# Attention with residual and layer norm on one core: splits of a coming quad's input in other graphs, and a bias add placed earlier on GpSimd

## Chip, cores and metric

The kernel runs on one core of one Trainium2 chip. The metric is the device time of one execution in microseconds (us). Some durations below are in nanoseconds where the profile has them so.

## The reference

For each of 128 graphs with 128 nodes and 384 features (12 heads of 32), all in float32:

```python
q = x @ Wq.T;  k = x @ Wk.T;  v = x @ Wv.T + bv          # split in 12 heads
a = softmax(where(all(a == 0), -inf, q k^T * 384**-0.5 + adj))   # NaN rows become 0
y = x + (a @ v) @ Wo.T + bo
out = (y - mean(y)) / sqrt(var(y) + 1e-5)                # over the 384 features
```

## The kernel before

The work goes in **quads** of four graphs, 32 of them, over tiles with two buffers (quad parity `p`). A hardware loop (`over_quads`) runs 15 times over a pair of quads, and the last pair is written out behind it. Each engine has its own instruction stream, in an order written out by hand, and semaphores order the engines among each other. Within a quad, `graph(j, p, b, ...)` for b = 0 to 3 is what an engine does in graph b's time. It works on several graphs at once: output projection, residual and layer norm of graph b, transposes of the probabilities of graph b+1, and softmax of graph b+2 (`later`). `nxt` is the next quad, `aft` the one after it.

The projections are exact to float32 by a split: a matrix is a high part (rounded, type fp32r) and a low part (the rest), and a product is three matmuls for each chunk of 128 features, hi·hi, hi·lo and lo·hi (`split_product`, L217 to L219). The input xT of a quad comes by one DMA into `xT_raw` (one buffer, three chunks). ScalarE makes the high parts (`keep_xT_hi`, L384), VectorE the low ones by a subtraction that reads `xT_raw` and `xT_hi` (`keep_xT_lo`, L501). Both are made for the quad `aft` during the present one.

The steps that matter here, by engine:

- **TensorE** (`quad`): ahead of `project_qk(*aft, 0, 1)`, near the end of graph 2's work, it waits for all three xT_lo and for `y_read` of graph 2, because that product writes the bank which the residual of graph 2 reads. Likewise `project_qk(*nxt, 3, 0)`, behind `project_v(j, p, 3, 1)`, waits for graph 0's `y_read`. `scores(*nxt, 0)` waits for the copy of product 5 (`qk_done`). Line L266 is `attend`, L241 `scores`, L254 the transposes.
- **ScalarE** (`graph`): exponentials (`exp_trio`, L402), copies of the products (`keep_qk`, L395), of the transposed probabilities (`keep_pT`, L409), of the attended values (`keep_oT_hi`, L415), and the high parts.
- **VectorE** (`graph`): `keep_oT_lo` (L562), the biased scores of four trios (`bias_trio`, L525), `keep_v` (L515), then `mask_half(0)`: `neg_sum` from `fold` (L537), reciprocal (L542), `live` (L547, reads two SBUF tiles), `row_scale` (L553, reads two SBUF tiles). Then `residual` (L569, gives `y_read`), `statistics`, `mean_variance`, `add_eps` (L582), `normalise` (L589, waits for GpSimd's `inv_std`), and `mask_half(1)`.
- **GpSimd** (`graph`): two `fold_half` (L661), which wait for the biased scores, `scale_half` 0 (L668), which waits for `row_scale`, `inverse_std` (L675), which waits for `add_eps`, `add_bo` (L654), which adds the output bias to the next graph's x and, except for the first graph of a quad, waits for nothing, and `scale_half` 1.
- **SyncE** issues all DMAs in one queue: output stores as they are done, and the loads of a coming quad between them.

In the notes below a "turn" is the passage from the end of the loop's body back to its start.

Of the kernel before, what the change touches and what calls it, by code (L numbers as in the profile page):

```python
# [28 lines left out]
QUAD = 4  # L29
# [16 lines left out]
def attention_kernel(nc, x, xT, adj, wq_t, wk_t, wv_t, wo_t, bv, bo, out):  # L46
# [7 lines left out]
    with ctx:  # L54
# [324 lines left out]
        @block.scalar  # L379
        def _(act):  # L380
            def keep_xT_hi(j, p, c):

                act.wait_ge(xT_loaded, 16 * (2 * j + p) + 16)
                nc.scalar.activation(xT_hi[p][:, c, :], xT_raw[:, c, :], ACT.Copy).then_inc(xT_hi_done, 1)  # L384

            def keep_w_hi(part):

                cols, factor = W_PARTS[part]
                act.wait_ge(w_loaded[cols.start // HIDDEN], 16)
                nc.scalar.activation(w_hi[:, :, cols], w_raw[:, :, cols], ACT.Copy, scale=factor)\  # L390
                    .then_inc(w_hi_done, 1)

            def keep_qk(j, p, k, turn):
                act.wait_ge(qk_psum, QK * (2 * j + p) + k + 1)
                nc.scalar.activation(qkT[p][:, k, :], turn_bank[turn][:, :], ACT.Copy)\  # L395
                    .then_inc(qk_done, 1)

            def exp_trio(j, p, b, trio):

                act.wait_ge(neg_a_done, 4 * (QUAD * (2 * j + p) + b) + trio + 1)  # L400
                for u in range(CHUNKS * trio, CHUNKS * (trio + 1)):
                    last = nc.scalar.activation(probs[b % 2][:, u, :], neg_a[b % 2][:, u, :], ACT.Exp,  # L402
                                                bias=neg_max[b % 2][:, u:u + 1], scale=-1.0,
                                                accum_out=row_sum[b % 2][:, u:u + 1])
                last.then_inc(exp_done, 1)

            def keep_pT(j, p, b, trio):
                act.wait_ge(pT_psum, 4 * (QUAD * (2 * j + p) + b) + trio + 1)
                nc.scalar.activation(pT[:, CHUNKS * trio:CHUNKS * (trio + 1), :],  # L409
                                     pT_bank[trio % 2][:, 0:HIDDEN].rearrange("p (c n) -> p c n", c=CHUNKS),  # L410
                                     ACT.Copy).then_inc(pT_done, 1)

            def keep_oT_hi(j, p, b):
                act.wait_ge(oT_psum, QUAD * (2 * j + p) + b + 1)
                nc.scalar.activation(oT_hi[:, :, :],  # L415
                                     turn_bank[ATTEND_BANK[b]][:, 0:HIDDEN].rearrange("p (c n) -> p c n", c=CHUNKS),
                                     ACT.Copy).then_inc(oT_hi_done, 1)

            def graph(j, p, b, has_next, has_after):
                nxt, aft = ahead(j, p, 1), ahead(j, p, 2)  # L420
                turn = 1 - ATTEND_BANK[b]
                more = b + 1 < QUAD or has_next
                more2 = b + 2 < QUAD or has_next
                if b == 1 and has_next:
                    keep_qk(*nxt, 3, turn)
                if b == 3 and has_after:
                    keep_qk(*aft, 0, turn)
                keep_oT_hi(j, p, b)
                if more:
                    keep_pT(*later(j, p, b, 1), 0)  # L430
                    keep_pT(*later(j, p, b, 1), 1)
                if more2:
                    exp_trio(*later(j, p, b, 2), 0)
                    exp_trio(*later(j, p, b, 2), 1)
                if b == 1 and has_next:
                    keep_qk(*nxt, 4, turn)
                if b == 3 and has_after:
                    keep_qk(*aft, 1, turn)
                if b == 2 and has_after:
                    keep_xT_hi(*aft, 2)  # L440
                if more2:
                    exp_trio(*later(j, p, b, 2), 2)
                if more:
                    keep_pT(*later(j, p, b, 1), 2)
                    keep_pT(*later(j, p, b, 1), 3)
                if more2:
                    exp_trio(*later(j, p, b, 2), 3)
                if b == 0 and has_after:
                    act.wait_ge(v_psum, QUAD * (2 * j + p) + QUAD)
                    keep_xT_hi(*aft, 0)  # L450
                if b == 1 and has_next:
                    keep_qk(*nxt, 5, turn)
                if b == 3 and has_after:
                    keep_qk(*aft, 2, turn)
                if b == 1 and has_after:
                    keep_xT_hi(*aft, 1)

            def quad(j, p, has_next, has_after):
                for b in range(QUAD):
                    graph(j, p, b, has_next, has_after)  # L460

            for c in range(CHUNKS):
                keep_xT_hi(0, 0, c)
            for part in range(4):
                keep_w_hi(part)
            for k in range(QK):
                keep_qk(0, 0, k, k % 2)
                if k < 2:
                    keep_w_hi(4 + k)
                if k >= CHUNKS:  # L470
                    keep_xT_hi(0, 1, k - CHUNKS)
            for trio in range(4):
                exp_trio(0, 0, 0, trio)
            keep_qk(0, 1, 0, 1)
            for trio in range(2):
                exp_trio(0, 0, 1, trio)
            keep_qk(0, 1, 1, 0)
            keep_pT(0, 0, 0, 0)
            keep_pT(0, 0, 0, 1)
            keep_qk(0, 1, 2, 1)  # L480
            keep_pT(0, 0, 0, 2)
            keep_pT(0, 0, 0, 3)
            for trio in range(2, 4):
                exp_trio(0, 0, 1, trio)
            over_quads(act, quad)
# [3 lines left out]
        def _(dve):  # L489
# [8 lines left out]
            def keep_xT_lo(j, p, c):  # L498

                dve.wait_ge(xT_hi_done, CHUNKS * (2 * j + p) + c + 1)  # L500
                nc.vector.tensor_tensor(xT_lo[p][:, c, :], xT_raw[:, c, :],  # L501
                                        xT_hi[p][:, c, :].bitcast(f32), ALU.subtract).then_inc(xT_lo_done, 1)
# [89 lines left out]
            def graph(j, p, b, has_next, has_after):  # L592
                nxt, aft = ahead(j, p, 1), ahead(j, p, 2)
                turn = 1 - ATTEND_BANK[b]
                more2 = b + 2 < QUAD or has_next
                keep_oT_lo(j, p, b)
                if more2:
                    for trio in range(4):
                        bias_trio(*later(j, p, b, 2), trio)
                if b == 1 and has_after:  # L600
                    keep_xT_lo(*aft, 0)
                if b == 0:
                    keep_v(j, p, 2, turn)
                if b == 2 and has_next:
                    keep_v(*nxt, 0, turn)
                if more2:
                    mask_half(*later(j, p, b, 2), 0)
                residual(j, p, b)
                statistics(j, p, b)
                mean_variance(j, p, b)  # L610
                add_eps(j, p, b)
                if b == 2 and has_after:
                    keep_xT_lo(*aft, 1)
                    keep_xT_lo(*aft, 2)
                if b == 0:
                    keep_v(j, p, 3, turn)
                if b == 2 and has_next:
                    keep_v(*nxt, 1, turn)
                normalise(j, p, b)
                if more2:  # L620
                    mask_half(*later(j, p, b, 2), 1)
# [27 lines left out]
        def _(pool):  # L649
# [7 lines left out]
            def fold_half(j, p, b, half):  # L657

                u = slice(HALF * half, HALF * (half + 1))
                pool.wait_ge(neg_a_done, 4 * (QUAD * (2 * j + p) + b) + 2 * half + 2)  # L660
                nc.gpsimd.tensor_tensor(fold[:, u, :], neg_a[b % 2][:, u, 0:N // 2],  # L661
                                        neg_a[b % 2][:, u, N // 2:N], ALU.add).then_inc(fold_done, 1)
# [15 lines left out]
            def graph(j, p, b, has_next):  # L678
                more2 = b + 2 < QUAD or has_next
                if more2:  # L680
                    fold_half(*later(j, p, b, 2), 0)
                    fold_half(*later(j, p, b, 2), 1)
                    scale_half(*later(j, p, b, 2), 0)
                inverse_std(j, p, b)
                if b + 1 < QUAD or has_next:
                    add_bo(*later(j, p, b, 1))
                if more2:
                    scale_half(*later(j, p, b, 2), 1)

# [50 lines left out]
```

## Time and profile before

| | us |
|---|---|
| median of 3 runs | 1311.45 (1310.1 to 1315.73) |
| profiled execution | 1316.24 |
| its span, first to last instruction | 1314.1 |
| TensorE matmul, busy | 1239.2 (94%) |
| VectorE, busy | 1047.5 (80%) |
| ScalarE, busy | 1025.6 (78%) |
| GpSimd, busy | 858.8 (65%) |

Busy shares say which engine has no room left, not which wait costs time. The granted TensorE clock was 0.991 of full over the span. A row of the timeline below begins with the start and the duration, both in us; the sum of the two is the instruction's end. A quad's time is about 39 us without the loop's turn and 41.36 us with it.

### The profile page before, as it was taken

The page shows a single profiled execution, that of the slowest core. Times are in us where ns is not written, and L with a number is a line of the kernel's source. Part 1 is how long each engine was busy: PE and PEld are TensorE (multiplying, and loading weights), DVE is VectorE, ACT ScalarE, POOL GpSimd, SP SyncE. Part 2 cuts the span into 40 slices and gives each one's busy share as a digit, 9 for nine tenths or more (in the row PEclk, how much of TensorE's full clock was granted, in tenths as well). Part 3 has the DMA queues.
Part 4 walks back from the last instruction along what each step waited for, and adds up shares of the span by engine and source line. Part 5 has one row for each costly group of instructions (what it writes and reads, how often), then busy time and mean ns, then how long its engine had stood idle before and what let it go on. Part 6 is the DMA issues. An engine that isn't in the chain of part 4 may idle for free.

```text
span 1314.1 us, 39607 instructions
## 1 busy us (share of the span) xinstructions
PE 1239.2 (94%) x11742; PEld 1059.2 (81%) x11742; DVE 1047.5 (80%) x5094; ACT 1025.6 (78%) x4007; POOL 858.8 (65%) x775
## 2 busy tenths in 40 slices
PE   9999999999999999999999999999998999999986
PEld 7887887878878787888878888788787887878875
DVE  5887887878788787887878878788787888878886
ACT  6887877868778777887878788788777887878784
POOL 2766766657667666676666666667666666667675
PEclk9999999999999999999999999999999999999998
DMA  6021202222122121122220221211222112212110
GB/s 220 22 82 67 74 27 80 74 67 74 33 74 74 67 80 59 42 80 70 71 75 26 80 75 66 75 43 64 75 72 75 54 46 81 74 67 74 33 43 31
DMA packets 58829, 87.64 MB, mean 67 GB/s; under 512 B 3680, under 2 KB 54624, under 8 KB 58720
## 3 DMA queue, kind: packets, MB, share of 16 engines
q1 hardware_dynamic: 58720, 86.65, 19.5%
q14 instruction: 97, 0.79, 0.2%
q8 instruction: 12, 0.20, 0.1%
HBM read 61.47 MB, written 25.17 MB: 66 GB/s over the span
## 4 chain that ended last, share of the span: by engine, by line
POOL 55%; issue 30%; PE 9%; DVE 2%; POOLq 2%; ACT 1%; DMA 0%; DVEq 0%; SPq 0%
POOL probs L668 24%; POOL fold L661 18%; POOL x_sb L654 9%; POOL inv_std L675 5%; PE turn_bank L217 2%; PE turn_bank L219 2%; PE turn_bank L218 2%; PE pT_bank L254 1%; PE score_bank L241 1%; PE turn_bank L266 1%; POOLq L660 1%; POOLq L667 1%; DVE neg_a L525 1%; ACT probs L402 0%; DMA xT_raw<-xT_dram 0%
## 5 line engine op out<-in xcount | busy, mean ns | idle before, releaser
L402 ACT ACTIVATE probs<-neg_a,neg_max 128x128 f32<-128x128 f32 x1536 | 596.4, 396 | 47.3 <-DVE neg_max L525 46.0
L668 POOL TENSOR_TENSOR probs<-probs,row_scale 128x768 f32<-128x768 f32 x256 | 376.5, 1471 | 193.6 <-DVE row_scale L553 193.6
L661 POOL TENSOR_TENSOR fold<-neg_a 128x384 f32<-128x384 f32 x256 | 271.0, 1059 | 195.3 <-DVE neg_max L525 195.3
L525 DVE CUSTOM_DVE_ANT_0 neg_a<-score_bank,adj_sb 128x128 f32<-128x128 f32 x1536 | 333.2, 285 | 0.0
L409 ACT ACTIVATE pT<-pT_bank 128x384 f32<-128x384 f32 x512 | 220.7, 484 | 105.3 <-PE pT_bank L254 105.0
L402 ACT ACTIVATION_READ_ACCUMULATOR probs<-neg_a,neg_max 128x1 f32 x1536 | 300.1, 195 | 0.0
L217 PE MATMUL turn_bank<-xT_hi,w_hi 128*128 128x512 f32 x576 | 241.0, 418 | 29.6 <-DVE xT_lo L501 28.7
L219 PE MATMUL turn_bank<-xT_hi,w_lo 128*128 128x512 f32 x576 | 228.1, 396 | 0.0
L218 PE MATMUL turn_bank<-xT_lo,w_hi 128*128 128x512 f32 x576 | 227.7, 395 | 0.0
L254 PE MATMUL pT_bank<-ident,probs 128*128 128x128 f32 x1536 | 219.8, 280 | 0.3 <-ACT pT L409 0.3
L254 PEld LDWEIGHTS pT_bank<-ident,probs 128*128 128x128 f32 x1536 | 176.1, 142 | 21.1 <-issue 1.2
L395 ACT ACTIVATE qkT<-turn_bank 128x512 f32<-128x512 f32 x192 | 113.8, 593 | 94.8 <-PE turn_bank L219 91.0
L589 DVE TENSOR_SCALAR out_sb<-y_sb,mean_var,inv_std 128x384 f32<-128x384 f32 x128 | 130.4, 1019 | 49.5 <-POOL inv_std L675 49.5
L562 DVE TENSOR_TENSOR oT_lo<-turn_bank,oT_hi 128x384 fp32r<-128x384 f32 x128 | 71.0, 555 | 121.3 <-ACT oT_hi L415 74.7
L217 PEld LDWEIGHTS turn_bank<-xT_hi,w_hi 128*128 128x128 f32 x576 | 108.5, 188 | 57.5 <-DVE xT_lo L501 39.4
L217 PE MATMUL turn_bank<-w_hi,oT_hi 128*128 128x384 f32 x384 | 132.2, 344 | 23.7 <-DVE oT_lo L562 23.7
L217 PE MATMUL turn_bank<-w_hi,xT_hi 128*128 128x384 f32 x384 | 141.2, 368 | 5.6 <-DVE v_sb L515 5.6
L654 POOL TENSOR_TENSOR x_sb<-x_sb,bo_sb 128x384 f32<-128x384 f32 x128 | 131.9, 1031 | 19.9 <-DMA x_sb<-x_dram 19.9
L537 DVE TENSOR_REDUCE neg_sum<-fold 128x6 f32<-128x384 f32 x256 | 138.9, 543 | 2.6 <-POOL fold L661 2.6
L219 PE MATMUL turn_bank<-w_hi,oT_lo 128*128 128x384 f32 x384 | 130.8, 341 | 0.0
L218 PE MATMUL turn_bank<-w_lo,oT_hi 128*128 128x384 f32 x384 | 130.4, 340 | 0.0
L218 PE MATMUL turn_bank<-w_lo,xT_hi 128*128 128x384 f32 x384 | 129.8, 338 | 0.0
(38 smaller groups left out, 2006.8 us busy)
## 6 DMA issues: line engine op xcount, KB each, us to landing
xT_raw<-xT_dram SPq DMA_DIRECT2D x32, 768.0 KB, 6.0
x_sb<-x_dram SPq DMA_DIRECT2D x32, 768.0 KB, 5.0
out_dram<-out_sb SPq DMA_DIRECT2D x128, 192.0 KB, 1.9
adj_sb<-adj_dram SPq DMA_DIRECT2D x32, 256.0 KB, 2.8
w_raw<-wq_t_dram SPq DMA_DIRECT2D x1, 576.0 KB, 5.6
w_raw<-wk_t_dram SPq DMA_DIRECT2D x1, 576.0 KB, 6.8
w_raw<-wv_t_dram SPq DMA_DIRECT2D x1, 576.0 KB, 7.9
w_raw<-wo_t_dram SPq DMA_DIRECT2D x1, 576.0 KB, 8.5
```

Of the source, the lines that this page charges most:

```text
L217: nc.tensor.matmul(dst, stat_hi(c), mov_hi(c), start=(c == 0), stop=False)
L218: nc.tensor.matmul(dst, stat_hi(c), mov_lo(c), start=False, stop=False)
L219: last = nc.tensor.matmul(dst, stat_lo(c), mov_hi(c), start=False, stop=(c == CHUNKS - 1))
L254: last = nc.tensor.transpose(pT_bank[r][:, c * N:(c + 1) * N], probs[b % 2][:, 3 * trio + c, :], ident[:, :])
L402: last = nc.scalar.activation(probs[b % 2][:, u, :], neg_a[b % 2][:, u, :], ACT.Exp, bias=neg_max[b % 2][:, u:u + 1], scale=-1.0, accum_ou ...
L409: nc.scalar.activation(pT[:, CHUNKS * trio:CHUNKS * (trio + 1), :], pT_bank[trio % 2][:, 0:HIDDEN].rearrange("p (c n) -> p c n", c=CHUNKS) ...
L525: last = nc.vector.tensor_tensor_reduce(out=neg_a[b % 2][:, u, :], in0=score_bank[trio][:, c * N:(c + 1) * N], in1=adj_sb[p][:, b, :], sca ...
L537: nc.vector.tensor_reduce(neg_sum[:, u], fold[:, u, :], AX.X, ALU.add).then_inc(mask_steps, 1)
L589: nc.vector.tensor_scalar(out_sb[:, b, :], y_sb[:, :], mean_var[:, 0:1], inv_std[:, 0:1], ALU.subtract, ALU.mult).then_inc(out_done, 1)
L654: nc.gpsimd.tensor_tensor(x_sb[p][:, b, :], x_sb[p][:, b, :], bo_sb[:, :], ALU.add)\
L661: nc.gpsimd.tensor_tensor(fold[:, u, :], neg_a[b % 2][:, u, 0:N // 2], neg_a[b % 2][:, u, N // 2:N], ALU.add).then_inc(fold_done, 1)
L668: nc.gpsimd.tensor_tensor(probs[b % 2][:, u, :], probs[b % 2][:, u, :], row_scale[:, u].unsqueeze(2).broadcast_to([P, HALF, N]), ALU.mult) ...
```

## The change

The high parts of chunks 1 and 2 are made one graph earlier on ScalarE: chunk 1 at the end of graph 0, straight behind chunk 0, and chunk 2 in the middle of graph 1. The low part of chunk 1 moves on VectorE from behind `add_eps` of graph 2 to behind `add_eps` of graph 1, and that of chunk 2 from there to the place ahead of `keep_v` in graph 2. On GpSimd `add_bo` moves from behind `inverse_std` to ahead of the first `scale_half`, right behind the two folds. No instruction is added or removed, and no DMA is changed.

```diff
 # ScalarE, graph()
-                if b == 2 and has_after:
+                if b == 1 and has_after:
                     keep_xT_hi(*aft, 2)
...
                 if b == 0 and has_after:
                     act.wait_ge(v_psum, QUAD * (2 * j + p) + QUAD)
                     keep_xT_hi(*aft, 0)
+                    keep_xT_hi(*aft, 1)
...
-                if b == 1 and has_after:
-                    keep_xT_hi(*aft, 1)
 # VectorE, graph()
                 if b == 1 and has_after:
                     keep_xT_lo(*aft, 0)
+                if b == 2 and has_after:
+                    keep_xT_lo(*aft, 2)
...
                 add_eps(j, p, b)
-                if b == 2 and has_after:
+                if b == 1 and has_after:
                     keep_xT_lo(*aft, 1)
-                    keep_xT_lo(*aft, 2)
 # GpSimd, graph()
                     fold_half(*later(j, p, b, 2), 1)
+                if b + 1 < QUAD or has_next:
+                    add_bo(*later(j, p, b, 1))
+                if more2:
                     scale_half(*later(j, p, b, 2), 0)
                 inverse_std(j, p, b)
-                if b + 1 < QUAD or has_next:
-                    add_bo(*later(j, p, b, 1))
                 if more2:
                     scale_half(*later(j, p, b, 2), 1)
```

## Rows read from the trace of the kernel before

**Rows 1.** Busy time by stretch, one quad: stretch, its length, busy time by engine, clock.
```profile
641.02:680.03 39.01, 38.05 (x367) 32.71 (x366) 32.86 (x160) 31.90 (x126) 27.23 (x26) 1.00 0.20 67
```
**Rows 2.** Waits over the whole span: total us, times, longest.
```profile
PEld turn_bank L217 <- DVE xT_lo L501: 39.4, 31, 1.3
PE turn_bank L217 <- DVE xT_lo L501: 28.7, 30, 1.0
PE turn_bank L217 <- DVE oT_lo L562: 23.7, 16, 2.0
```
**Rows 3.** Timeline, graph 2 of that quad: TensorE and VectorE around the xT_lo wait.
```profile
664.54 0.55 DVE L515 TENSOR_TENSOR v_sb<-turn_bank,bv_sb 128x384 f32<-128x384 f32 x1
...
665.87 0.56 DVE L569 TENSOR_TENSOR y_sb<-turn_bank,x_sb 128x384 f32<-128x384 f32 x1
...
667.44 1.29 DVE L501 TENSOR_TENSOR xT_lo<-xT_raw,xT_hi 128x512 fp32r<-128x512 f32 x2
667.49 0.34 PE L219 MATMUL turn_bank<-w_hi,xT_lo 128*128 128x384 f32 x1
...
668.79 0.50 PE L217 MATMUL turn_bank<-xT_hi,w_hi 128*128 128x512 f32 x1 [0.95 <-DVE xT_lo L501]
```
**Rows 4.** Single lines, whole span: duration ns min/median/max.
```profile
L589 DVE TENSOR_SCALAR out_sb<-y_sb,mean_var,inv_std x128: 478/1132/1164, 45.9 to 1311.2; 128x384 f32<-128x384 f32 x128
L553 DVE TENSOR_TENSOR row_scale<-live,inv_sum x256: 165/166/170, 27.8 to 1299.8; 128x6 f32<-128x6 f32 x128
```
**Rows 5.** Timeline, graph 1 of that quad: VectorE, GpSimd, ScalarE and scores.
```profile
655.41 0.69 DVE L501 TENSOR_TENSOR xT_lo<-xT_raw,xT_hi 128x512 fp32r<-128x512 f32 x1
...
655.58 1.39 POOL L661 TENSOR_TENSOR fold<-neg_a 128x384 f32<-128x384 f32 x1 [0.25 <-DVE neg_max L525]
...
656.60 0.40 DVE L547 TENSOR_TENSOR live<-neg_max,neg_sum 128x6 f32<-128x6 f32 x1
...
657.03 0.17 DVE L553 TENSOR_TENSOR row_scale<-live,inv_sum 128x6 f32<-128x6 f32 x1
...
657.28 1.47 POOL L668 TENSOR_TENSOR probs<-probs,row_scale 128x768 f32<-128x768 f32 x1 [0.31 <-DVE row_scale L553]
657.31 0.56 DVE L569 TENSOR_TENSOR y_sb<-turn_bank,x_sb 128x384 f32<-128x384 f32 x1
...
658.78 0.15 DVE L582 TENSOR_SCALAR var_eps<-mean_var 128x1 f32<-128x1 f32 x1
...
659.01 0.55 POOL L675 TENSOR_TENSOR inv_std<-var_eps,minus_half 128x1 f32<-128x1 f32 x1 [0.27 <-DVE var_eps L582]
...
659.53 1.02 POOL L654 TENSOR_TENSOR x_sb<-x_sb,bo_sb 128x384 f32<-128x384 f32 x1
...
659.60 1.16 DVE L589 TENSOR_SCALAR out_sb<-y_sb,mean_var,inv_std 128x384 f32<-128x384 f32 x1 [0.66 <-POOL inv_std L675]
...
660.01 0.60 ACT L395 ACTIVATE qkT<-turn_bank 128x512 f32<-128x512 f32 x1
660.50 0.62 ACT L384 ACTIVATE xT_hi<-xT_raw 128x512 fp32r<-128x512 f32 x1
...
660.68 0.54 DVE L537 TENSOR_REDUCE neg_sum<-fold 128x6 f32<-128x384 f32 x1
660.73 0.95 PE L241 MATMUL score_bank<-qkT 32*128 32x128 f32 x24
```
**Rows 6.** Timeline, graph 3 and, behind the loop's turn, graph 0 of the next quad.
```profile
675.71 1.01 POOL L661 TENSOR_TENSOR fold<-neg_a 128x384 f32<-128x384 f32 x1 [0.25 <-DVE neg_max L525]
...
677.44 0.56 DVE L569 TENSOR_TENSOR y_sb<-turn_bank,x_sb 128x384 f32<-128x384 f32 x1 [0.41 <-PE turn_bank L219]
...
688.04 1.01 POOL L661 TENSOR_TENSOR fold<-neg_a 128x384 f32<-128x384 f32 x1 [0.25 <-DVE neg_max L525]
...
689.20 0.56 DVE L569 TENSOR_TENSOR y_sb<-turn_bank,x_sb 128x384 f32<-128x384 f32 x1
...
690.16 0.40 PE L217 MATMUL turn_bank<-xT_hi,w_hi 128*128 128x512 f32 x1
```

## The prediction

> **What bounds the kernel now.** I read the busy time of a stretch first. One quad without a turn of the loop takes 39.01 us and TensorE is busy for 38.05 of it at a full clock; GpSimd, with 27.23, is far from full [rows 1]. The chain that ended last goes mostly through GpSimd, and the longest waits are GpSimd's own; I set them aside, since an idle GpSimd costs nothing unless someone waits for it. So the question is what TensorE waits for. The waits answer: 30 times, once a quad, 28.7 us for xT_lo, the low parts of the coming input; its weight loads waited 1.27 us each (39.4/31). The other wait of size, 23.7 us in 16 pieces for oT_lo, falls right behind the turn of the loop [rows 2].
>
> Where xT_lo costs time is graph 2's stretch [rows 3]. TensorE starts the last matmul of the V projection at 667.49, and the next product could follow 0.17 later, at 667.66. VectorE does the residual at 665.87 to 666.43, then two xT_lo from 667.44 to 668.73, and TensorE starts at 668.79, 0.06 behind. With the slower first matmul (0.50 for about 0.40) that is 1.23 us lost a quad. The product behind it waits for two things, xT_lo and y_read, that is, this same residual. Residual is early by 1.2 us today. That is the slack which the change must not use up.
>
> **A lock between VectorE and GpSimd.** The same stretch of graph 1 shows what decides here [rows 5]. `live` reads two tiles of SBUF; it starts at 656.60, takes 0.40, and ends at 657.00, just after GpSimd's fold ended at 656.97. That fold took 1.39 where the one of graph 3 takes 1.01 [rows 6]: it began under xT_lo, which also reads two tiles. Normalise starts at 659.60 and ends at 660.76, 0.21 after add_bo's end at 660.55. Alone it takes 0.478 (its shortest), yet its median is 1.132 [rows 4]. So today every add_bo is paid for by VectorE, hidden in normalise's length.
>
> The Trainium skill ("SBUF — State Buffer", section "Who interferes with whom") says that a VectorE instruction with two SBUF inputs, or in a two-port mode, and a GpSimd instruction that reads SBUF exclude each other, the later one waiting for the whole of the earlier. No row shows this for row_scale, which never met a GpSimd instruction. By that rule row_scale is held for all of add_bo, as I take it below from `live`; it speaks against a part of this change. With the rule the sum is the one of -13.0 us below; without it, that of the second rival.
>
> **The change, part by part.**
>
> (a) ScalarE. The conversions keep their number. The one of chunk 1 goes to graph 0's end, the one of chunk 2 to the middle of graph 1. In graph 1 it stands ahead of the copy of qk product 5, which starts at 660.01; scores of the next graph start at 660.73, 0.12 after that copy ended. A conversion takes 0.62, with 0.10 of it under its neighbour (660.50, and the copy before it ends at 660.61), so 0.52 net: the copy ends at 661.13 and scores start near 661.19, 0.46 late [rows 5]. TensorE would then reach the xT_lo product at about 668.12 rather than 667.66. The oT_hi behind is not later, since the conversion that stood between is gone. At graph 0's end ScalarE waits for TensorE; nothing there.
>
> (b) VectorE in graph 1. fold ends at 656.97, add_bo follows at once for 1.02, to 657.99, and row_scale, otherwise due at 657.03, ends 0.03 later, at 658.02. VectorE overlaps neighbours by 0.08 (normalise ends 660.76, neg_sum starts 660.68), so residual starts at 657.94, 0.63 late. xT_lo of chunk 1 follows var_eps, 1.57 behind residual's start: 659.51. scale_half 0 runs from 658.10 to 659.57 and inv_std comes after it, so xT_lo (0.69) is first. inv_std is then held to 660.20, and as the fold ended 0.87 after xT_lo's end with a length of 1.01, I let it end 0.41 after: 660.61. Normalise starts 0.04 on, now with GpSimd idle: 0.48, to 661.13. neg_sum starts at 661.05 where it was 660.68. Graph 1 ends 0.37 late: residual to neg_sum takes 3.11 instead of 3.37, since xT_lo lies in the 0.66 in which VectorE sat idle and normalise gives back more than the hold of inv_std costs, but residual itself was 0.63 late [rows 5].
>
> (c) VectorE in graph 2. xT_lo of chunk 2 now stands where keep_v starts today, 664.54. As in graph 1, fold ends 1.56 behind the start of that xT_lo (655.41 to 656.97). add_bo runs from 1.57 to 2.59; `live` is due at 1.66, so it too is held, to 2.62; row_scale 2.65 to 2.82; residual at 2.74. Today it is 1.33 behind that point (664.54 to 665.87). So residual starts 0.37 + 1.41 = 1.78 late, at 667.65, and ends at 668.21 [rows 3, 5]. TensorE waits for y_read and starts at 668.27 instead of 668.79. **0.52 us a quad**, not 1.23: the wait changes its name from xT_lo to y_read. Since TensorE would only have arrived at 668.12, the late scores of (a) are covered; without that cover they cost 0.46. Over 30 quads: -15.6 us.
>
> (d) Without an xT_lo, the stretch from residual to neg_sum shrinks from 3.37 (657.31 to 660.68) to 2.69: scale_half ends 1.63 behind residual's start, inv_std 2.25, normalise runs 2.29 to 2.77. That is 0.68 back. In graph 3 residual would start 0.98 behind the fold's end (0.01 + 1.02 + 0.03 - 0.08): 676.72 + 0.98 = 677.70 for 677.44, so VectorE is through 0.42 sooner [rows 5, 6]. At the turn of the loop TensorE waits for VectorE [rows 2], so 15 times 0.42: -6.3 us.
>
> (e) Behind that turn, graph 0. fold ends at 689.05, so residual starts at 690.03 for 689.20 and ends at 690.59. TensorE's next product, at 690.16, needs it: 690.65, and 0.10 for a cold first matmul, so 0.59 lost [rows 6]. 15 times: +8.9 us. In the other quads of a pair VectorE comes into graph 0 earlier by (d)'s gain, and I take no loss.
>
> (f) SyncE's queue: the conversions are done sooner, but the next load of xT stands behind output stores, so no transfer moves. Probs scaled by half 0 come later by about 1 us; their transposes stand a graph's scores behind. Nothing.
>
> Sum: -15.6 - 6.3 + 8.9 = **-13.0 us**. The profiled execution took 1316.24 us (span 1314.1 and 2.1 around it), so 1303.2 on its terms; it lay 4.8 above the median of the three runs. On the median: 1311.45 - 13.0 = 1298.5.
>
> **Bounds of the unknown.** The price of add_bo ahead of row_scale lies between 0 (no lock for such small operands; row_scale shows 165 to 170 ns always [rows 4]) and 1.2 a graph (add_bo's 1.02 and `live` losing its turn as well). I take 0.98 behind the fold's end, as `live` is the nearest row.
>
> **Rivals.**
> - *The lock costs a step more everywhere.* `live` of graphs 0, 1 and 3 is also passed by add_bo: 0.20 more each. A quad then gains 0.32, the turn 0.22, and graph 0 loses 0.79: -9.6 - 3.3 + 11.9 = -1.0, 1310 us. For: live and row_scale stand close to the fold's end in every graph. Against: `live` got in right behind the fold today.
> - *No lock on row_scale.* Then y_read comes at about 666.9 (0.60 for xT_lo on 666.43, little from graph 1) and TensorE runs on at 668.12: -1.23 + 0.46 = -0.77 a quad, and the turn gives 0.5 (0.68 less some 0.2 by which scale_half, now behind add_bo, makes inv_std later): -23.1 - 7.5 = -30.6, 1281 us. For: TensorE's whole wait is then gone. Against: `live`'s 0.40.
> - *Slower: normalise isn't shortened.* If its 1.13 isn't add_bo's doing, 0.68 comes back in each graph: a quad loses 0.16, the turn 0.26, graph 0 0.59: +4.8 + 3.9 + 8.9 = +17.6, 1329 us. A pair of quads gains 0.87 in my sum and the missing part counts three times in it, so it decides from 0.29 us on. Against: 0.478 once, with GpSimd idle.
>
> **How the numbers follow.** My case 0.45 (own range 1292 to 1305), the costlier lock 0.2 (1305 to 1315), no lock 0.15 (1278 to 1288), slower 0.12, others 0.08. From 1280 to 1315 all but 2 in 10 are held. What three or five rounds can tell from no change is about 0.5%, 6.6 us. Faster: nearly all of my case and no lock, a little of the rest, 0.58. Same: mostly the costlier lock, 0.27. Slower: 0.15.
>
> **What would show it.** Normalise's median near 0.48 us; row_scale's far above 0.17, about 1.0; TensorE's waits for xT_lo gone and one for y_sb in their place near 0.6 us a quad, and one behind each turn; scores of the next graph late for qkT. Wrong it would be if row_scale stays at 0.17, if normalise stays above 1 us, or if scores' delay meets a TensorE that waits for nothing later.

## Result and the profile after

The changed kernel takes 1297.09 us in the median of 6 runs (1293.95 to 1303.86), the kernel before 1312.93 in its 6. The ratio is 0.9889, 95% interval [0.9857, 0.9921]: 1.1% faster. A second measurement of the same kernel (below) gave 0.9852 [0.983, 0.9874]. The forecast was -13.0 us, or 1298.5; measured are -15.8 us by these medians and -20.5 by the second measurement's (1293.82 against 1314.31). The profiled execution took 1296.31 us (span 1294.2) against 1316.24 (span 1314.1).

Waits of the changed kernel over the whole span (total us, times, longest):

```profile
DVE oT_lo L561 <- issue: 49.2, 14, 5.8
...
PE turn_bank L217 <- DVE oT_lo L561: 19.2, 16, 3.6
...
PE score_bank L241 <- ACT qkT L395: 10.3, 31, 0.7
...
PE turn_bank L217 <- DVE y_sb L568: 3.5, 14, 0.3
...
PEld turn_bank L217 <- DVE xT_lo L500: 2.1, 1, 2.1
```

The 30 waits of TensorE for xT_lo, 28.7 us [rows 2], are gone; the one that is left is a weight load's, at 8.6 us from the start, ahead of the loop. In their place stand a wait of scores for qkT once a quad, 0.30 to 0.36 each but for the first, and a small one for y_sb, 0.25 each, behind the turns of the loop. The wait for oT_lo at the turn fell from 23.7 to 19.2 us, and to 15.7 in the second measurement; the median of its 16 pieces fell from 1.58 to 0.92 and 0.98. In the first line, "issue" means that nothing the profile shows held VectorE: it is VectorE's own pause at 14 turns, 46.5 us before, longest 3.8.

Single lines of the changed kernel (duration ns min/median/max), to be read beside [rows 4]. VectorE's lines are one number lower than before: L588 is normalise, L552 row_scale, L546 `live`.

```profile
L588 DVE TENSOR_SCALAR out_sb<-y_sb,mean_var,inv_std x128: 473/479/483, 46.6 to 1291.3; 128x384 f32<-128x384 f32 x128
L552 DVE TENSOR_TENSOR row_scale<-live,inv_sum x256: 165/166/936, 27.7 to 1281.1; 128x6 f32<-128x6 f32 x128
L546 DVE TENSOR_TENSOR live<-neg_max,neg_sum x256: 123/166/917, 27.5 to 1280.9; 128x6 f32<-128x6 f32 x128
```

Normalise is never held again. row_scale and `live`, six elements in each partition, now last up to 0.94 us: row_scale in graphs 0, 1 and 3 (0.86 to 0.94), `live` in graph 2 (0.90 to 0.92). Medians hide it, as half the calls (the second halves) meet an idle GpSimd; the maxima show it.

Timeline of the changed kernel, graph 1 of a quad, to be laid beside [rows 5]. VectorE and GpSimd are shown, and of TensorE only the starts of `attend` and scores:

```profile
604.94 0.69 DVE L500 TENSOR_TENSOR xT_lo<-xT_raw,xT_hi 128x512 fp32r<-128x512 f32 x1
605.10 1.40 POOL L661 TENSOR_TENSOR fold<-neg_a 128x384 f32<-128x384 f32 x1 [0.25 <-DVE neg_max L524]
...
606.12 0.40 DVE L546 TENSOR_TENSOR live<-neg_max,neg_sum 128x6 f32<-128x6 f32 x1
606.46 1.01 POOL L654 TENSOR_TENSOR x_sb<-x_sb,bo_sb 128x384 f32<-128x384 f32 x1
606.56 0.94 DVE L552 TENSOR_TENSOR row_scale<-live,inv_sum 128x6 f32<-128x6 f32 x1
607.41 0.55 DVE L568 TENSOR_TENSOR y_sb<-turn_bank,x_sb 128x384 f32<-128x384 f32 x1
607.57 1.47 POOL L668 TENSOR_TENSOR probs<-probs,row_scale 128x768 f32<-128x768 f32 x1
...
608.98 0.69 DVE L500 TENSOR_TENSOR xT_lo<-xT_raw,xT_hi 128x512 fp32r<-128x512 f32 x1
609.11 0.96 POOL L675 TENSOR_TENSOR inv_std<-var_eps,minus_half 128x1 f32<-128x1 f32 x1
...
609.38 0.86 PE L266 MATMUL turn_bank<-pT,v_sb 128*32 128x128 f32 x24
...
610.11 0.48 DVE L588 TENSOR_SCALAR out_sb<-y_sb,mean_var,inv_std 128x384 f32<-128x384 f32 x1 [0.44 <-POOL inv_std L675]
610.51 0.54 DVE L536 TENSOR_REDUCE neg_sum<-fold 128x6 f32<-128x384 f32 x1
...
610.58 0.61 PE L241 MATMUL score_bank<-qkT 32*128 32x128 f32 x12 [0.34 <-ACT qkT L395]
```

add_bo ends at 607.47 and row_scale 0.03 later. Residual starts 0.91 behind the fold's end (606.50 to 607.41; forecast 0.97), and residual to neg_sum takes 3.10 (forecast 3.11). xT_lo gets in ahead of inv_std and holds it to 0.96. Scores start 1.20 behind `attend`, where it was 0.83 (659.90 to 660.73): 0.37 late. The row of `attend` before, and of ScalarE the instruction ahead of the copy of product 5; then ScalarE's two rows after:

```profile
659.72 0.21 ACT L402 ACTIVATION_READ_ACCUMULATOR probs<-neg_a,neg_max 128x1 f32 x1
659.90 0.86 PE L266 MATMUL turn_bank<-pT,v_sb 128*32 128x128 f32 x24
```
```profile
609.77 0.20 ACT L402 ACTIVATION_READ_ACCUMULATOR probs<-neg_a,neg_max 128x1 f32 x1
609.86 0.59 ACT L395 ACTIVATE qkT<-turn_bank 128x512 f32<-128x512 f32 x1
```

Graph 2 of the same quad, where the wait for xT_lo stood [rows 3]:

```profile
615.88 1.01 POOL L654 TENSOR_TENSOR x_sb<-x_sb,bo_sb 128x384 f32<-128x384 f32 x1
...
616.01 0.91 DVE L546 TENSOR_TENSOR live<-neg_max,neg_sum 128x6 f32<-128x6 f32 x1
...
617.04 0.56 DVE L568 TENSOR_TENSOR y_sb<-turn_bank,x_sb 128x384 f32<-128x384 f32 x1
...
617.35 0.34 PE L219 MATMUL turn_bank<-w_hi,xT_lo 128*128 128x384 f32 x1
617.74 0.47 PE L217 MATMUL turn_bank<-xT_hi,w_hi 128*128 128x512 f32 x1
```

The last matmul of the V projection starts at 617.35, and the product behind it at 617.74, 0.22 later than the usual step of 0.17 would have it, and 0.14 behind residual's end at 617.60. In both quads of a pair it starts 0.15 behind residual's end in the median, so residual is what it waits for; the waits above show none here, as the idle time is this short. Here `live` starts 0.13 after add_bo and is the one that is held.

Graph 0 behind a turn [rows 6]:

```profile
675.51 1.02 POOL L654 TENSOR_TENSOR x_sb<-x_sb,bo_sb 128x384 f32<-128x384 f32 x1
...
675.64 0.91 DVE L552 TENSOR_TENSOR row_scale<-live,inv_sum 128x6 f32<-128x6 f32 x1
...
676.48 0.54 DVE L568 TENSOR_TENSOR y_sb<-turn_bank,x_sb 128x384 f32<-128x384 f32 x1
...
677.08 0.50 PE L217 MATMUL turn_bank<-xT_hi,w_hi 128*128 128x512 f32 x1 [0.24 <-DVE y_sb L568]
```

To see where the time went I took the start of each `attend` on TensorE's timeline and the distance to the next one, for all pairs of quads of the loop; the medians, in us, with the experiments told below. The first column holds the turn's wait and graph 0, the others named the two graphs 2. The five columns not shown lie between 8.90 and 9.94 in every kernel and change by 0.04 at most.

```
kernel                  attend 0->1,   attend 2->3,   attend 2->3,
                        behind turn    first quad     second quad
before                  12.55          11.19          11.19
changed                 12.38          10.62          10.42
changed, again          12.42          10.63          10.42
e1_bias_only            12.43          11.93          11.93
e2_splits_only          12.39          10.30          10.30
e3_hi2_late             12.46          10.60          10.30
e4_splits_hi2_late      12.39          10.12           9.97
e5_bias_graph3          11.85          10.13           9.97
e6_bias_one_column      11.69          10.31          10.30
```

The changed kernel gains 0.57 and 0.77 in graph 2 and about 0.15 at the turn: 1.5 us for a pair, 22 us for 15 pairs. The two profiled spans differ by 19.9 us. Medians leave out two turns of the changed kernel's profile that took 14.39 and 15.41 us in this column, and the profiled execution before was 3.3 us above the median of the six runs, so the columns tell where time went better than how much of it the kernel lost.

### The profile page after: what moved, and what is told of

It is laid out like the page before. It is cut to its first block, busy times and chain, and to the rows that moved or that the text cites. A ratio compares the mean times of both kernels' runs of the same rounds, so it can differ in the third digit from the quotient of the medians.

```text
span 1294.2 us, 39607 instructions
## 1 busy us (share of the span) xinstructions
PE 1236.7 (96%) x11742; PEld 1053.8 (81%) x11742; DVE 1072.3 (83%) x5094; ACT 1019.9 (79%) x4007; POOL 861.6 (67%) x775
## 3 DMA queue, kind: packets, MB, share of 16 engines
q1 hardware_dynamic: 58720, 86.65, 19.9%
## 4 chain that ended last, share of the span: by engine, by line
POOL 55%; issue 30%; PE 8%; ACT 2%; DVE 2%; POOLq 2%; DMA 0%; DVEq 0%; SPq 0%
POOL probs L668 24%; POOL fold L661 17%; POOL x_sb L654 9%; POOL inv_std L675 5%; PE turn_bank L217 2%; PE turn_bank L219 2%; PE turn_bank L218 2%; ACT probs L402 1%; PE pT_bank L254 1%; PE score_bank L241 1%; PE turn_bank L266 1%; POOLq L660 1%; POOLq L667 1%; ACT pT L409 0%; DVE neg_a L524 0%
## 5 line engine op out<-in xcount | busy, mean ns | idle before, releaser
L661 POOL TENSOR_TENSOR fold<-neg_a 128x384 f32<-128x384 f32 x256 | 283.1, 1106 | 178.9 <-DVE neg_max L524 178.9
L217 PE MATMUL turn_bank<-w_hi,oT_hi 128*128 128x384 f32 x384 | 131.4, 342 | 19.2 <-DVE oT_lo L561 19.2
L241 PE MATMUL score_bank<-qkT 32*128 32x128 f32 x3072 | 122.3, 288 | 10.3 <-ACT qkT L395 10.3
```

Of the source, the lines that this page charges most:

```text
L217: nc.tensor.matmul(dst, stat_hi(c), mov_hi(c), start=(c == 0), stop=False)
L241: last = nc.tensor.matmul(score_bank[r][:, c * N:(c + 1) * N], qkT[p][row, c, tok], qkT[p][row, CHUNKS + c, tok], start=True, stop=True)
```

## Experiments

Theory: the earlier xT_lo brings the gain, and add_bo ahead of row_scale takes part of it back, since GpSimd's add holds VectorE's instructions with two SBUF inputs. The expectations below call this the lock theory. First rival: the shorter normalise is what brings the gain or makes room for the xT_lo. Second rival: the late copy of qk product 5 limits the changed kernel. Each was timed in five rounds.

**Only the bias add moved.** Against the kernel before:

```diff
+                if b + 1 < QUAD or has_next:
+                    add_bo(*later(j, p, b, 1))
+                if more2:
                     scale_half(*later(j, p, b, 2), 0)
                 inverse_std(j, p, b)
-                if b + 1 < QUAD or has_next:
-                    add_bo(*later(j, p, b, 1))
```

> Only GpSimd's add_bo is moved; both splits stay where they were. Lock theory: normalise falls to 0.48 us, row_scale or live is held about 0.9 us, residual of graph 2 comes 0.8 us later with both xT_lo still behind it, so TensorE's wait for xT_lo grows from 0.96 to about 1.7 us a quad. The turn of the loop gives back about 0.45, graph 0 behind it costs about 0.3. Sum about +0.75 x 30 - 2 = +20 us, some 1.5% slower than before. Rival (the gain of the whole change comes from the shorter normalise): about 1% faster than before.

Measured: 1334.7 us, ratio 1.0161 [1.0144, 1.0178]: **slower by 1.6%**. Its waits, and its groups of instructions by line (busy us, mean ns of one, idle before):

```profile
PE turn_bank L217 <- DVE xT_lo L501: 50.8, 30, 1.7
```
```profile
L553 DVE TENSOR_TENSOR row_scale<-live,inv_sum 128x6 f32<-128x6 f32 x256 | 134.3, 525 | 8.7
L589 DVE TENSOR_SCALAR out_sb<-y_sb,mean_var,inv_std 128x384 f32<-128x384 f32 x128 | 61.1, 478 | 51.4 <-POOL inv_std L675 51.4
```

TensorE's wait for xT_lo is 1.69 a quad, as expected. Normalise fell from 1019 ns in the mean to 478 and the kernel still lost: that the shorter normalise brings the gain, the first half of the first rival, is out.

**Only the splits moved.** Against the changed kernel add_bo goes back behind `inverse_std`.

```diff
-                if b + 1 < QUAD or has_next:
-                    add_bo(*later(j, p, b, 1))
                 if more2:
                     scale_half(*later(j, p, b, 2), 0)
                 inverse_std(j, p, b)
+                if b + 1 < QUAD or has_next:
+                    add_bo(*later(j, p, b, 1))
```

> Only the splits are moved; add_bo stays behind inverse_std. Lock theory: the xT_lo wait goes (-1.23 us a quad), normalise stays at 1.13, scores of the next graph are 0.4 late for the copy of product 5, y_read of graph 2 at about 667.4 on the old scale is early enough. About -0.75 x 30 = -22 us, nothing at the turn: 1.5% faster than before, the same as the whole change within 0.5%. Rival (the shorter normalise is needed to make room for the xT_lo in graphs 1 and 2): no faster than before, since VectorE becomes later than TensorE in graph 2.

Measured: 1287.76 us, 0.9804 [0.9787, 0.9821]. By line:

```profile
L588 DVE TENSOR_SCALAR out_sb<-y_sb,mean_var,inv_std 128x384 f32<-128x384 f32 x128 | 144.3, 1128 | 41.2 <-POOL inv_std L675 39.4
L552 DVE TENSOR_TENSOR row_scale<-live,inv_sum 128x6 f32<-128x6 f32 x256 | 42.5, 166 | 8.7
```

Faster than before by more than the whole change, so the shorter normalise isn't needed to make room. "The same as the whole change within 0.5%" missed: it is 0.5 to 0.9% faster (0.9804 against 0.9852 and 0.9889, intervals apart from both), 6 to 11 us. Graph 2 takes 10.30 in both quads, 0.32 and 0.12 less than with the change: 15 times 0.44 is 6.6 us. The late residual still costs in the changed kernel, even where the trace shows no named wait: its product starts 0.38 and 0.23 us behind the matmul ahead of it in the two quads, here 0.18 in both, and its first matmul lasts 0.47 for 0.40.

**The high part of chunk 2 made later.** Against the changed kernel:

```diff
-                if b == 1 and has_after:
-                    keep_xT_hi(*aft, 2)
                 if more2:
                     exp_trio(*later(j, p, b, 2), 2)
...
                 if b == 3 and has_after:
                     keep_qk(*aft, 2, turn)
+                if b == 1 and has_after:
+                    keep_xT_hi(*aft, 2)
```

> The whole change, but the high part of chunk 2 is made at the end of graph 1, behind the copy of product 5, where the one of chunk 1 was made before. If the late copy is what limits the changed kernel: the 0.3 us wait of scores for qkT goes in each quad, up to -10 us against the change. If y_read of graph 2 is as near as I worked out, it takes its place and nearly nothing is gained: TensorE waits for y_sb in graph 2 about 0.3 us a quad instead, at most -3 us.

Measured: 1295.97 us, 0.9875 [0.9851, 0.9899], the same as the change. Its waits no longer have scores for qkT among the recurring ones, and have instead:

```profile
PE turn_bank L217 <- DVE y_sb L568: 8.5, 30, 0.3
```

14 waits for y_sb (3.5 us) have become 30 (8.5 us). The copy's delay was covered by residual's, and the second rival is out for the changed kernel: two delays lie over each other. Only in the second quad of a pair, where residual's is the smaller, graph 2 is 0.12 shorter (10.30 for 10.42), 1.8 us in all and less than the runs' scatter.

**Both: splits moved, high part of chunk 2 late, add_bo where it was.** The last two edits together.

> Splits moved with the high part of chunk 2 behind the copy of product 5, and add_bo left where it was. Lock theory: neither the wait for qkT nor one for y_sb or xT_lo in graph 2 is left: -1.2 us a quad, -37 us, about 2.7% faster than before and some 1.3% faster than the change. Rival (shorter normalise is needed): no faster than the change, with waits for y_sb or xT_lo of some tenths of a us.

Measured: 1282.36 us, 0.976 [0.9743, 0.9778]. Graph 2 takes 10.12 and 9.97, 1.07 and 1.22 less than before; in the second quad that is the whole of the 1.23 worked out for the wait. In the first quad TensorE comes to the end of the V projection 0.16 later than in the second; where it loses this was not followed up. Without the hold by add_bo the late high part is worth 5.4 us (1287.76 to 1282.36); with it, it was worth nothing that can be measured. I expected 2.7% and got 2.4. What is left is the turn:

```profile
PE turn_bank L217 <- DVE oT_lo L561: 24.5, 16, 2.5
```

**add_bo early in graph 3 alone.** Against the last kernel:

```diff
                 if more2:
+                    if b == 3:
+                        add_bo(*later(j, p, b, 1))
                     scale_half(*later(j, p, b, 2), 0)
                 inverse_std(j, p, b)
-                if b + 1 < QUAD or has_next:
+                if b < 3:
                     add_bo(*later(j, p, b, 1))
```

> As e4_splits_hi2_late, but in graph 3 alone add_bo stands ahead of the first scale_half. The lock theory says: normalise of graph 3 falls from 1.13 to 0.48 us, row_scale or live of graph 3 is held to the end of add_bo, VectorE comes some 0.45 us sooner to the turn of the loop, where TensorE waits for oT_lo (24.5 us in 16 pieces). No hold falls into graph 0, 1 or 2. So 15 x 0.45 = 7 us faster than e4_splits_hi2_late, about 1275 us, 2.9% faster than before. Rival (the turn's wait is a fixed time of fetching instructions, whatever VectorE does ahead of it): the same as e4_splits_hi2_late.

Measured: 1273.69 us, 0.9706 [0.9679, 0.9733]: **2.9% faster than before**, and the best of all. It is 8.7 us less than the last one; against the kernel before, timed beside each, it is 0.5 points, 7 us. The turn:

```profile
PE turn_bank L217 <- DVE oT_lo L561: 14.8, 16, 1.3
```

The wait for oT_lo fell by 9.7 us and the column behind the turn from 12.39 to 11.85. The turn's wait is not a fixed one: it falls as VectorE gets to the turn earlier. VectorE's own pause there stays, 3.0 to 3.5 us in this kernel.

**The bias added to one column in 384.** The changed kernel with add_bo in its new place and next to no length; the bias of the other 383 columns is left out.

```diff
-                nc.gpsimd.tensor_tensor(x_sb[p][:, b, :], x_sb[p][:, b, :], bo_sb[:, :], ALU.add)\
+                nc.gpsimd.tensor_tensor(x_sb[p][:, b, 0:1], x_sb[p][:, b, 0:1], bo_sb[:, 0:1], ALU.add)\
```

> The changed kernel with the bias added to one column in 384 (the rest of the bias is left out), so add_bo stands in the same place and takes little. Lock theory: row_scale and live are back at 0.17 us, normalise stays at 0.48, the wait for y_sb ahead of product 3 behind the turn goes, the wait for qkT stays. From e2_splits_only (1287.8 us) less 0.45 to 0.6 x 15 for the shorter normalise at the turn: about 1280 us, 17 us less than the changed kernel. Rival (row_scale is long because of its place in the order, not by add_bo's length): row_scale stays at 0.9 us and the time at about 1297 us.

Measured: 1275.23 us, 0.9704 [0.9686, 0.9721]. By line:

```profile
L588 DVE TENSOR_SCALAR out_sb<-y_sb,mean_var,inv_std 128x384 f32<-128x384 f32 x128 | 61.2, 478 | 37.8 <-POOL inv_std L675 33.8
L552 DVE TENSOR_TENSOR row_scale<-live,inv_sum 128x6 f32<-128x6 f32 x256 | 42.5, 166 | 8.7
```

row_scale is back at 166 ns in the same place of the order, so add_bo's length was its 0.9. That is 18.6 us less than the changed kernel timed beside it (1293.82), where 17 were expected: this is what the length of add_bo costs in its new place, with all that it holds or puts back. Its column behind the turn is 11.69, 0.69 below the change's.

**The changed kernel once more.**

> The changed kernel once more, unaltered, beside the others on the same chip. Both theories: 1.1 to 1.3% faster than before, about 1297 us.

Measured: 1293.82 us, 0.9852 [0.983, 0.9874], a little better than expected; its interval overlaps the first one's.

## Why the prediction was right

The forecast was -13.0 us with 1292 to 1305 as its own range, and both measurements, 1297.09 and 1293.82, lie in it. The mechanism is the forecast one: the wait moved from xT_lo to y_read, and add_bo's hold moved from normalise to row_scale and `live`. The sum was too small by 3 to 7.5 us, in the terms told below.

**The wait to look at.** Right. The wait for xT_lo is gone in every kernel with the earlier splits, and where neither scores nor residual are late (e4_splits_hi2_late and e5_bias_graph3, second quad) graph 2's column falls by 1.22 us, against 1.23 worked out from the rows.

**(a) Scores late for the copy of product 5.** Right in mechanism and cover: scores are 0.37 late for 0.46. The working was loose: scores stood 0.12 behind the copy in the row and 0.06 in the sum, and the copy was put back by 0.52, where it came only 0.37 later against `attend` (0.48 behind it for 0.11). It had begun 0.29 behind the start of the instruction ahead of it and now begins 0.09 behind, so part of the conversion fell into time in which ScalarE had waited. e3_hi2_late shows the delay covered in the change, e4_splits_hi2_late that it costs once the cover is gone.

**(b) Graph 1.** Right to a few hundredths in the first quad of a pair: residual to neg_sum 3.10 for 3.11. In the second quad inv_std came before xT_lo and wasn't held (0.55 us for 0.96), and the stretch took 2.81.

**(c) Graph 2.** Right in kind: y_read took the place of xT_lo. Mis-sized: 0.57 and 0.77 us a quad measured where 0.52 was forecast, 20 us over the loop in place of 15.6. In the first quad the product starts 0.53 earlier (0.52 forecast), but partly by luck, for two errors met: each of the two holds on the way was 0.06 shorter than I had it, since add_bo is recorded as starting 0.04 before the fold's end and not 0.01 behind it, and TensorE starts 0.15 behind residual's end and not 0.06. The second quad escapes the hold of inv_std; its residual comes 0.20 earlier, and 15 times that is 3 of the missing 4.5 us. The sign named for this part, a wait for y_sb of about 0.6 us in each quad, did not show: scores are late too, and what is left between the two is 0.2 us or less.

**(d) and (e) The turn and graph 0.** Forecast was +0.17 us a pair together, measured -0.17 and, in the second measurement, -0.13, so the sign was missed. The two parts can be read one by one. e5_bias_graph3 has (d)'s gain with its hold in graph 3 and not (e)'s price: 0.54 below e4_splits_hi2_late (0.42 forecast). The changed kernel has both and lies 0.53 above e5_bias_graph3, which is (e)'s price (0.59 forecast); residual starts 0.92 behind the fold's end for 0.98. The two nearly cancel, and the rest of the fall is there with the splits alone (12.39 for 12.55), where the forecast had nothing. The turn itself scatters: VectorE's longest wait there was 3.8 us before and 5.8 in the changed kernel, so a tenth or two a pair in this column is not settled.

**The rivals.** The costlier lock and no lock are both excluded by the rows: `live` got in ahead of add_bo in graphs 0, 1 and 3 of every quad of the loop (0.17, 0.40 and 0.17 us), and row_scale was held. What no lock would have given is about what e6_bias_one_column shows, 1275 us; the rival said 1281. The slower case fell with normalise at 0.479 in the median and 0.483 at most. It lives on in another form: without the earlier splits, the bias add alone does lose 1.6%.

**What the forecast didn't say.** The change is two edits of opposite sign. Moving the splits is worth 2.0% (2.4% with the high part of chunk 2 placed better); moving add_bo takes a quarter to nearly half of the 2.0 back, and where its place was changed in one graph alone, graph 3, it was of use; graphs 0, 1 and 2 were not tried one by one. (d) had its gain at the turn and (e) its price in graph 0 side by side; to take the one and leave the other was one condition on b away.

## What to carry to other kernels

Where GpSimd and VectorE hold each other, moving GpSimd's work doesn't remove the hold but chooses its victim: look which VectorE instruction it lands on and who waits for that one. Read the maxima of short instructions, not the medians, to find a hold. When a wait goes, work out which semaphore comes next at the same place before counting the gain, and test the parts of a change alone: here one of two paid for the other.

## What the runs showed of the hardware

An instruction of six elements in each partition (0.166 us alone) took up to 0.94 us beside a GpSimd add of 1.01 us, and went back to 0.165 to 0.169 when that add had one column. neg_sum, which reads one SBUF tile, began 94 times while a GpSimd add or multiply was running in the changed kernel and never took more than 0.554 us, where its median is 0.545. The Trainium skill ("SBUF — State Buffer", section "Who interferes with whom") has it that a VectorE instruction with two SBUF inputs is shut out for the whole of a GpSimd instruction that reads SBUF and was first; the trace agrees, row_scale ending 0.03 us behind add_bo. One pair of rows doesn't show a hold for the whole: in the second quad of 14 pairs xT_lo, which reads two tiles, starts 0.12 us into inv_std (0.55 us, one element in each partition) and takes its usual 0.69, with 0.20 us of idle time ahead of it. In these runs the one that already waits gets in when the other's instruction ends: `live`, recorded as starting at 606.12, ended at 606.52, 0.02 behind the fold, although add_bo is recorded from 606.46 on. It took 0.398 to 0.405 us in graph 1 of every quad of the loop, while `live` of graph 2, which starts 0.13 behind add_bo, took 0.90 to 0.92. Normalise, 1.132 us in the median before, takes 0.479 when no GpSimd instruction runs beside it; it reads one SBUF tile and two single columns, and no run here separates what in it is held.
